# A decoder kernel's Mamba layer: how rows of C reach all partitions, which PSUM banks hold the products, and where the skip term is added

## The reference

```
u   = silu(causal_conv(x @ in_w_u) + conv_b)            # 256 inner features
x_dbl = u @ xproj_w                                     # 8 rows for dt, 16 for B, 16 for C
dt  = softplus(x_dbl[:8] @ dt_w + dt_b)
h_t = exp(dt*A) * h_{t-1} + dt * B_t * u_t              # 16 states for each feature
y_t = sum_n h_t[n] * C_t[n]  +  u * D
out = (y * silu(z)) @ out_w
```

## Time and profile before

| | us |
|---|---|
| median of 3 runs | 2780.08 (2778.74 to 2786.33) |
| the profiled execution: its time | 2784.18 |
| its span, first to last instruction | 2782.4 |
| stretch of the Mamba steps, 54 to 1103 | 1049.0 |
| DVE busy in that stretch | 969.87 |
| PE busy in that stretch | 857.71 |

### The profile page before, as it was taken

One profiled execution on the slowest core, in us unless ns is written; L12 is line 12 of the kernel. 1 busy time (PEld: TensorE's weight loads), 2 busy tenths in 40 slices (PEclk: granted clock), 3 DMA queues, 4 the chain that ended last, 5 costly groups with the idle time before them and its releaser, 6 DMA issues. The chain is left out here.

```text
span 2782.4 us, 46621 instructions
## 1 busy us (share of the span) xinstructions
PE 2415.8 (87%) x14880; PEld 1576.7 (57%) x14880; DVE 2111.5 (76%) x3021; ACT 1491.9 (54%) x2699; POOL 1192.6 (43%) x868
## 2 busy tenths in 40 slices
PE   2788888877888886999599998799999989978997
PEld 1333333333333332777488886566666767757776
DVE  2999999999999997777455555688888857764555
ACT  3767677777777663566322222566666656642010
POOL 4676766666677665333200001355555432231000
PEclk9899999999999998899699999899999989988999
DMA  3000000000000000100000000000000010000000
GB/s 85 1 0 1 1 0 1 0 1 0 0 0 1 0 0 24 43 11 11 21 1 1 0 0 6 1 1 0 0 0 0 0 50 11 11 3 0 12 8 12
DMA packets 35413, 22.17 MB, mean 8 GB/s; under 512 B 22710, under 2 KB 34016, under 8 KB 34800
## 3 DMA queue, kind: packets, MB, share of 16 engines
q1 hardware_dynamic: 35312, 20.98, 2.9%
HBM read 18.87 MB, written 2.10 MB: 8 GB/s over the span
## 5 line engine op out<-in xcount | busy, mean ns | idle before, releaser
L796 POOL TENSOR_TENSOR m_hc<-m_h,m_cs 128x1024 f32<-128x1024 f32 x256 | 603.1, 2359 | 316.3 <-DVE m_h L715 315.0
L715 DVE TENSOR_TENSOR_SCAN m_h<-m_da,m_pdb 128x1024 f32<-128x1024 f32 x256 | 585.1, 2286 | 24.5 <-DVE m_pdb L670 5.5
L453 PE MATMUL m_py<-m_hc,ident 128*128 128x512 f32 x1024 | 511.6, 624 | 8.2 <-DVE m_y L679 6.1
L609 ACT ACTIVATE m_da<-m_dt,m_aneg 128x508 f32<-128x508 f32 x512 | 338.2, 710 | 13.6 <-POOL m_dt L765 10.5
L670 DVE TENSOR_TENSOR m_pdb<-m_du,m_pdb 128x1024 f32<-128x1024 f32 x256 | 314.8, 1230 | 39.5 <-POOL m_du L772 11.4
L453 PEld LDWEIGHTS m_py<-m_hc,ident 128*128 128x128 f32 x1024 | 199.8, 199 | 232.5 <-issue 184.5
L624 ACT ACTIVATE m_cs<-m_pc 128x512 f32<-128x512 f32 x256 | 150.8, 589 | 247.6 <-PE m_pc L443 247.5
L439 PE MATMUL m_pdb<-m_bcrow,m_sel 96*128 96x512 bf16 x256 | 102.4, 400 | 146.8 <-DVE m_h L715 145.3
L1403 ACT ACTIVATE c_act_of<-c_pg 128x512 f32<-128x512 f32 x144 | 86.3, 599 | 236.0 <-PE c_pg L212 236.0
L1049 ACT ACTIVATE x_prT<-x_pt 77x512 f32<-77x512 f32 x256 | 137.8, 586 | 134.1 <-PE x_pt L951 133.7
L1771 POOL TENSOR_TENSOR d_pr<-d_pr,d_rden 128x512 f32<-128x512 f32 x128 | 133.1, 1040 | 177.1 <-DVE d_rden L1702 177.1
(11 more groups left out here) (261 smaller groups left out, 5487.7 us busy)
## 6 DMA issues: line engine op xcount, KB each, us to landing
cw_gu<-in_C_gu SPq DMA_DIRECT2D x1, 2304.0 KB
x<-in_x SPq DMA_DIRECT2D x8, 256.0 KB, 5.1
fw_w<-in_F_w SPq DMA_DIRECT2D x1, 2048.0 KB
out_x<-x SPq DMA_DIRECT2D x8, 256.0 KB, 2.3
bm_mrow<-in_B_mrow SPq DMA_DIRECT2D x1, 1232.0 KB, 6.2
x_ctxT<-in_B_ctxT SPq DMA_DIRECT2D x32, 38.5 KB, 1.8
x_mask<-in_B_mrow SPq DMA_DIRECT2D x32, 38.5 KB, 2.8
x_ctxT<-in_E_ctxT SPq DMA_DIRECT2D x32, 38.5 KB, 1.8
```

Source lines behind the costliest of these rows:

```text
L453: ins = mm(py[:, c, :], S.ident[:, :], hc[n % BUF][:, place(n, c), :], start=n == 0, stop=n == NS - 1)
L609: A_(dst, src, ACT.Exp, scale=aneg[:, d, c, n:n + 1]).then_inc(s["da_ready"], 1)
L715: V.tensor_tensor_scan(h[n % BUF][:, way], da[n % BUF][:, d:d + CH * GT][:, way], pdb[:, b:b + 2, :].rearrange("p c t -> p (c t)")[:, way] ...
L796: P.tensor_tensor(hc[n % BUF][:, :, :], h[n % BUF][:, :].rearrange("p (c t) -> p c t", c=CH), bc(cs[n % BUF][:, :], 1, CH), ALU.mult).then ...
```

## The change

Three parts, made together.

1. The C row no longer goes through PE, PSUM and ACT. The projection gives the 16 C rows once more, in fp32, as rows 104 to 119 of its output. ACT copies them beside the dt rows to `frow` in SBUF. SP, idle before, issues one transfer per step: one row of `frow`, 512 fp32 in one SBUF partition (104 + n), is read 128 times and written to the 128 partitions of `cs`. It waits for `frow_ready` once per unit and for `hc_ready` of four steps before; POOL waits for the transfer on `c_in`. The C matmul, its bank `pc` and the ACT copy are gone.
2. With the freed bank `pdb` has four banks: even steps use the pair 0 and 1, odd steps the pair 2 and 3. The product no longer waits for the scan before it, and `place` is gone.
3. The skip term: `skip` holds diagonal matrices with D; two matmuls per unit start the sum in `py`. `sum_up` becomes two plain copies on ACT at n = 4, and POOL's `gate` moves from n = 4 to n = 5.

```diff
-    NROW = 3 * 2 * NS + DR
+    NROW = FP_ROWS + DR + NS
-        sel = A.sb("sel", [96, 2 * NS, 128], BF16)
+        sel = A.sb("sel", [96, NS, 128], BF16)
+        skip = A.sb("skip", [128, 2, CH, 128])
-        dtrow = A.sb("dtrow", [128, GT])
+        frow = [A.sb(f"frow{d}", [128, GT]) for d in range(2)]
-        pdb = A.ps("pdb", [128, 3, GT])
-        pc = A.ps("pc", [128, GT])
+        pdb = A.ps("pdb", [128, 4, GT])
...
+            @block.sync
+            def _(sp):
...
+                def scan(g, d, nxt):
+
+                    u = 2 * g + d
+                    sp.wait_ge(s["frow_ready"], u + 1)
+                    for n in range(NS):
+                        N = NS * u + n
+                        if due(N + 1 - BUF):
+                            sp.wait_ge(s["hc_ready"], N + 1 - BUF)
+                        row = FP_ROWS + DR + n
+                        sp.dma_start(cs[n % BUF][:, :], bc(frow[d][row:row + 1, :], 1, 128)
+                                     ).then_inc(c_in[n % BUF], 16)
...
-                    if due(N):
-                        pe.wait_ge(s["c_ready"], N)
-                    mm(pc[:, :], sel[:, NS + n, :], bcrow[d][:, :],
-                       start=True, stop=True).then_inc(s["c_mm"], 1)
...
+                        for c in range(CH):
+                            mm(py[:, c, :], skip[:, d, c, :], us[d][:, c, :], start=True, stop=False)
...
-                        act.wait_ge(s["c_mm"], N + 1)
-                        if due(N + 1 - BUF):
-                            act.wait_ge(s["hc_ready"], N + 1 - BUF)
-                        A_(cs[n % BUF][:, :], pc[:, :], ACT.Copy).then_inc(s["c_ready"], 1)
+                        if n == 4 and not (isinstance(u, int) and u == 0):
+                            sum_up(u - 1, 1 - d)
...
+                def sum_up(u, d):
+
+                    act.wait_ge(s["y_mm"], NS * (u + 1))
+                    if due(u):
+                        act.wait_ge(s["ys_ready"], u)
+                    for c in range(CH):
+                        A_(y1[:, c, :], py[:, c, :], ACT.Copy).then_inc(s["y1_ready"], 1)
...
-                    if due(N):
-                        dve.wait_ge(s["h_ready"], N)
-                    out = pdb[:, 1::-1, :] if n % 2 == 0 else pdb[:, 1:3, :]
+                    out = pdb[:, 1::-1, :] if n % 2 == 0 else pdb[:, 3:1:-1, :]
...
-                            if n == 3:
-                                sum_up(u - 1, 1 - d)
...
-                        if n == 4 and not first:
+                        if n == 5 and not first:
                             gate(u - 1, 1 - d)
                         pool.wait_ge(s["h_ready"], N + 1)
-                        pool.wait_ge(s["c_ready"], N + 1)
+                        pool.wait_ge(c_in[n % BUF], c_count(u, n))
```

More of the change, by code:

```diff
@@ L31 @@
 DI, NS, DR, TAPS = 256, 16, 8, 4
+FP_ROWS = 3 * 2 * NS
 CH = DI // 128
@@ L335, in mamba_layer, with c_count @@
         names = """prep stats rstd xh_ready xres_ready lnT_mm lnT_ready z_mm z_raw u_mm us_ready zs_ready
-            row_mm row_hi row_rest row_mid row_low row_ready dtrow_ready dt_mm dt_abs dt_relu dt_soft dt_ready
-            du_ready b_mm c_mm c_ready da_ready db_ready h_ready hc_ready y_mm y1_ready ys_ready o_mm
+            row_mm row_hi row_rest row_mid row_low row_ready frow_ready dt_mm dt_abs dt_relu dt_soft dt_ready
+            du_ready skip_ready b_mm da_ready db_ready h_ready hc_ready y_mm y1_ready ys_ready o_mm
             x_ready seg_zero aexp_ready""".split()
         s = {n: A.sem(n) for n in names}
+        c_in = [A.sem(f"c_in{k}") for k in range(BUF)]
+        def c_count(u, n):
+            return 16 * (NS // BUF * u + n // BUF + 1)
         def row_bank(n):
             return 2 * (n % 2)
-        def place(n, c):
-            return c if n % 2 == 0 else 1 - c
         with nc.Block() as block:
@@ L374, in drive, with front @@
                 group(NG - 1, 1, last=True)
+            @block.sync
+            def _(sp):
+                def front(g, d, at=None):
+                    pass
+                def scan(g, d, nxt):
[8 more added lines that the diff above has]
+                                     ).then_inc(c_in[n % BUF], 16)
+                drive(sp, front, scan, [0])
             @block.tensor
@@ L440, in spread, with add_state @@
                        start=True, stop=True).then_inc(s["b_mm"], 1)
[L441 to L446 removed]
+                def add_state(u, n, d):
                     pe.wait_ge(s["hc_ready"], NS * u + n + 1)
                     if n == 0:
+                        pe.wait_ge(s["us_ready"], CH * (u + 1))
                         if due(CH * u):
                             pe.wait_ge(s["y1_ready"], CH * u)
+                        for c in range(CH):
+                            mm(py[:, c, :], skip[:, d, c, :], us[d][:, c, :], start=True, stop=False)
                     for c in range(CH):
[L453 to L454 removed]
+                        ins = mm(py[:, c, :], S.ident[:, :], hc[n % BUF][:, c, :],
+                                 start=False, stop=n == NS - 1)
                     ins.then_inc(s["y_mm"], 1)
@@ L485, in scan @@
                         if n >= LAG:
-                            add_state(u, n - LAG)
+                            add_state(u, n - LAG, d)
                         elif not first:
-                            add_state(u - 1, NS + n - LAG)
+                            add_state(u - 1, NS + n - LAG, 1 - d)
                         if n == 8 and not first:
@@ L492, in scan @@
                         for n in range(NS - LAG, NS):
-                            add_state(u, n)
+                            add_state(u, n, d)
                         project_out(u, d, nxt)
@@ L605, in decay @@
                     for c in range(CH):
-                        at = place(n, c) * GT
+                        at = c * GT
                         dst = da[n % BUF][:, at:at + GT].rearrange("p (i t) -> p i t", t=T)[:, :, 1:T]
@@ L628, in scan @@
                             gate_in(u, d)
+                    if not nxt:
+                        sum_up(u, d)
                 drive(act, front, scan, par)
@@ L640, in _ @@
                 V.tensor_copy(sel[:, :, :], bc(W.sel32[:, :], 2, 128)).then_inc(s["prep"], 1)
+                for d in range(2):
+                    for c in range(CH):
+                        V.tensor_scalar(skip[:, d, c, :], S.ident[:, :], W.dskip[:, d, c:c + 1], None, ALU.mult
+                                        ).then_inc(s["skip_ready"], 1)
                 dve.wait_ge(s["aexp_ready"], 1)
@@ L2153, in layout @@
         rows = f[r + "xproj_w"]
-        spread = np.concatenate([rows[DR:], rows[DR:], rows[DR:], rows[:DR]]).T
+        spread = np.concatenate([rows[DR:], rows[DR:], rows[DR:], rows[:DR], rows[DR + NS:]]).T
         a[q + "xprojT"] = spread.reshape(CH, 128, -1).transpose(1, 0, 2)
```

33 lines of the change are left out of this document (14 added, 19 removed).

## The result

The changed kernel takes 3898.43 us (median of 4 runs, 3893.03 to 3900.53), the kernel before 2783.2 us (4 runs, 2778.74 to 2786.68): ratio 1.4003, interval 1.398 to 1.4026. It is 40% slower. The forecast was 4255 us with a range of 3400 to 5000. The profiled execution took 3900.53 us, its span is 3898.7 us.

The account below looks back on a forecast made before the run. The prediction took DVE to bound the Mamba layer, at 3.71 us a step. Transfers of 9.79 us would delay the last `hc` by 1474 us: 2784.2 + 1474 = 4258 us profiled, 4255 us as median, range 3400 to 5000.

Parts of the forecast that it names:

- one engine's rate: C transfers out of one partition get only what one DMA engine takes: 9.8 us each; 9.3 to 12.1 us had chance 0.72.
- hidden: Rival in the Mamba steps: transfers land in time, DVE remains the bound, 2718 us; chance 0.14 for a gain above 0.3%.
- 256 x 9.79 = 2506 us back to back: Mamba steps: the 256 C transfers follow one another without gaps from 57.1 us, so the last `hc` starts at 2563.
- The 62 us of DVE: Mamba steps: DVE's total saving, 48 - 3 + 17 = 62 us, if the C rows come in time.
- the wait: DVE, between scan and product: dropping it saves about 0.19 us at 255 neighbours, 48 us, less 3.
- the skip term: Leaving DVE, between product and scan, it saves 1.13 us, 15 times: 17 us.
- C off PE and ACT: 256 ACT copies of 589 ns and as many matmuls go; worth 0, as neither engine sets the period.
- the 3 us that the prediction took off: DVE at L659, one step per unit: no gain from the dropped wait there, 15 such steps, 3 us.
- if that cover were gone, it would cost 19 us: Skip term on PE and ACT: without their waits for DVE as cover, its added work would cost 16 x 1.2 = 19 us.
- The signs listed: Trace signs for the Mamba steps if right: landings 30 to 40 us, about 27 GB/s, PE's clock 0.50 for much of them.
- a new wait eats the gain: Rival: transfers hidden, but ACT waits for the later `gate`, 16 to 62 us; chance 0.02 within 0.3%, 0.02 slower.
- slower than one engine: Rival: reads of one partition from 16 sides disturb each other, 19.6 us a transfer, 6765 us; 0.04 for over 12.1 us.

Follow-up runs that it names:

- e10_two_in_flight: The changed kernel with SP issuing C's transfers so that two are in flight in place of four: 4079.16 us, ratio 1.4664.
- e1_ports: The changed kernel with its 16 C rows stored in another order, so that consecutive transfers read partitions 4 apart: 2948.46 us, ratio 1.0597.
- e4b_same: The changed kernel with each C row kept twice, in partitions 16+n and 48+n, each copy serving 64 of the 128 destinations: 4039.8 us, ratio 1.4519.
- e2_hbm: The changed kernel with the 16 C rows of a unit written to HBM once and the 256 transfers reading them from there: 2710.62 us, ratio 0.9745.
- e9_conly: The kernel before with only C moved off PE and ACT, its rows read from HBM by transfers: 2777.75 us, ratio 0.9988.
- e7_skip: The kernel before with only the third part of the change, the skip term on PE and ACT: 2806.68 us, ratio 1.0086.
- e8_both: The changed kernel with reordered C rows and two copies of each row, each serving half of the destinations: 2734.01 us, ratio 0.9829.

## Why the prediction was right, and where it was off

**The direction and the cause held.** The term that was to decide, the rate at which one row comes out of SBUF, was costed between 0.6 and 12.1 us a transfer, and the end that was taken, one engine's rate, was nearly it: 9.8 us within a group of four partitions. No row of before showed a transfer out of one partition, as the prediction says; that end was chosen by an argument, and that a sixteenth of the 424 GB/s is also the rate of one port was nowhere derived from the rows. To that extent the close value was luck, though the Trainium skill's 27.2 GB/s (SBUF — State Buffer, "Door 1: The DMA port swizzle") stood behind it. The trace shows the chain that was forecast: landings, then `hc`, then the scan. The rival "hidden" (0.14) fell by the landings of 27.9 us.

**The step that was mis-sized** is "256 x 9.79 = 2506 us back to back". Measured are 256 x 8.40 = 2150 us, 356 us less, practically the whole distance between 4255 and 3898. The transfers aren't strictly one behind the other. Where two of them read out of different ports they overlap: in the changed kernel that happens once in four states, and the windows show up to 65 GB/s there. e10_two_in_flight took part of the overlap away (9.11 us), e1_ports made it the rule (4.68 us).

**The mechanism was named a little too narrowly.** The prediction spoke of one partition that all engines ask. e1_ports reads one partition with each transfer too, and e4b_same reads two and gains nothing. The limit is the port behind a group of partitions. The prediction itself gave the figure of the Trainium skill for it (the same section), 27.2 GB/s, and the windows show 23 to 31 outside the overlaps, 26.8 at 9.8 us a transfer.

**The 62 us of DVE** were said to be unseen in the forecast and to come in the hidden case, with 2718 us. e2_hbm, where the transfers are hidden, measured 2710.62. By parts: the wait 49.6 and 50.0 (48 - 3 forecast), the skip term 17.1 and 17.6 (17), C off PE and ACT about 3 by the ratio of e9_conly, 1 to 6 with its interval (0 forecast). The subtraction beside POOL behaved as the earlier trace rows let expect: L700 now takes 1752 ns where L659 took 1554, 3 us over 16 of them, the 3 us that the prediction took off:

```profile
L659 DVE TENSOR_TENSOR m_rest<-m_rest,m_bcrow 32x512 f32<-32x512 f32 x16 | 24.9, 1554 | 1.8 <-ACT m_bcrow L558 1.3
```

**"Worth 0" for C was right only alone.** The prediction costed the three parts one by one and added them. e7_skip shows that they don't add: without C's removal the skip term's move costs 26 us, with it it saves 17. It had said "if that cover were gone, it would cost 19 us" and held the cover to be ample, by totals of idle time. The totals were ample; at states 7 to 9, where ACT and PE do the next unit's front, it was not there.

**The signs listed** came out: POOL's idle time ended by the DMA, DVE's by `hc`, scans still 2286 ns. Landings were 27.9 us instead of 30 to 40, the rate 31 instead of 27 GB/s, and PE's granted clock 0.72 on average instead of 0.50 for much of the stretch.

**The rival "a new wait eats the gain"** is excluded for this kernel by e2_hbm: the later gate costs nothing there that shows. The "slower than one engine" case fell too: the longest distances of `hc` in the rows above are 10.1 us, not 19.6.

**Open.** e1_ports reaches 57 GB/s, two ports' worth, though its waits allow four transfers out of four ports. By its landings, 15.3 us at one every 4.68 us, about three are on the way. Why these don't give three times the rate was not tried. The 68 GB/s of e8_both, at a DMA share of 0.92, are no ceiling by themselves: e2_hbm, bound by DVE, asks for no more than 70. That the transfer engines drift apart and the leading ones start on the next port is the picture that fits e10_two_in_flight; the runs show that what is in flight decides, not the drift itself. That the ACT copy's lateness alone makes e7_skip's PE late was read from its trace and not isolated.

## What to carry to other kernels

Before replacing a compute broadcast by a transfer, ask where the source lies: bytes read out of one group of four partitions came at some 27 GB/s here (31 with the overlaps) although all 16 engines were kept busy (0.88), so a 2-KB row to 128 partitions occupied the source for 9.8 us, while the same transfer out of HBM landed 3.4 us after its issue. If it must come from SBUF, spread copies and consecutive rows over groups of partitions that don't share a port, and keep several such transfers in flight. And cost a moved instruction by the idle time of its new engine at that very place in the program, not by the engine's total, once with and once without the other parts of the change.

## What the runs showed of the hardware that was not expected

- Reads of single partitions out of different ports do overlap, though one port alone gives some 27 GB/s: 31 GB/s in order, 57 with rows four partitions apart, 68 with two copies as well.
- Rereading one 2-KB row of HBM 128 times is cheap: 70 GB/s of such transfers keep the DMA engines busy 0.23 of the time, with landings of 3.4 us.
- A wait on DVE that is met the moment the instruction before it ends still costs 0.19 us a time (49.6 us over 255).
- SP's issue of a transfer took 0.43 us before, 0.47 us with two in flight (e10_two_in_flight) and 0.45 us with four allowed out of HBM (e2_hbm), but 9.09 us at the median in the changed kernel, where four are allowed out of a slow source. Nothing else stood in SP's queue here; that a load behind such an issue would come late follows from that, but no run has one.

```profile
L392 SPq DMA_DIRECT2D m_cs<-m_frow x256: 574/9086/9890, 54.5 to 2178.7; - x128
```

The row gives the duration of SP's 256 issues in the changed kernel, shortest, median and longest in ns, and the first and last start.
